# Rounding, remainders, routing steps and the final sums of a mixture-of-experts kernel put in other places

## The reference, cut to what matters

```python
x = x + L0_attn_ref(_layernorm(x), w_qkva, gamma)      # x: 4 x 1024 x 256, float32
#   h = rmsnorm(x, gamma); q, kv, a = split(h @ w_qkva.T, 3); y_t = sigmoid(a_t) * y_{t-1} + kv_t; q * y
x = x + L0_ffn_ref(_layernorm(x), router_w, w_gate, w_up, w_down, sw_gate, sw_up, sw_down)

def _L0_ffn_ref(x, ...):                                # 7 routed experts, top 2; hidden 1024
    logits = x_flat @ router_w.T                        # x_flat: 4096 x 256
    top_vals, top_idx = jax.lax.top_k(logits, 2)
    top_w = jax.nn.softmax(top_vals, axis=-1)
    combine = jnp.sum(jax.nn.one_hot(top_idx, 7) * top_w[..., None], axis=1)
    routed_out = _swiglu(x_flat, w_gate, w_up, w_down)  # down(silu(x @ gate) * (x @ up)), each expert
    mixed = jnp.einsum('end,ne->nd', routed_out, combine)
    return mixed + jnp.mean(_swiglu(x_flat, sw_gate, sw_up, sw_down), axis=0)
```

## Time and profile before

| | |
|---|---|
| device time, median of 3 runs | 1114.69 us (1114.1 to 1115.27) |
| the profiled execution | 1114.16 us, its span 1112.4 us |
| mean granted TensorE clock | 0.965 |
| busy: PE, PEld | 1019.9 us (92%), 882.9 us (79%) |
| busy: DVE, ACT, POOL | 637.9 us (57%), 477.9 us (43%), 407.6 us (37%) |
| DMA over the span | 155.08 MB, mean 139 GB/s |

### The profile page before, as it was taken

One profiled execution on the slowest core, in us unless ns is written; L12 is line 12 of the kernel. 1 busy time (PEld: TensorE's weight loads), 2 busy tenths in 40 slices (PEclk: granted clock), 3 DMA queues, 4 the chain that ended last, 5 costly groups with the idle time before them and its releaser, 6 DMA issues.

```text
span 1112.4 us, 16252 instructions
## 1 busy us (share of the span) xinstructions
PE 1019.9 (92%) x5757; PEld 882.9 (79%) x5757; DVE 637.9 (57%) x1037; ACT 477.9 (43%) x778; POOL 407.6 (37%) x258
## 2 busy tenths in 40 slices
PE   7999999998999999999999999999999688888897
PEld 6788978877989978777877887787779677777776
DVE  7997677876333353464346444644553655656566
ACT  4554342231233244354435443543454444455474
POOL 3234000002101443554455345634653666445300
PEclk9999999999999999999999999999999988888899
DMA  8324110002865744424443444344434555343544
GB/s 293 95 77 113 41 28 10 20 1 82 255 246 179 269 158 166 152 85 160 165 142 94 165 160 141 95 165 165 133 96 168 175 214 198 132 155 118 180 143 142
DMA packets 145907, 155.08 MB, mean 139 GB/s; under 512 B 75321, under 2 KB 134210, under 8 KB 138690
## 3 DMA queue, kind: packets, MB, share of 16 engines
q1 hardware_dynamic: 139120, 136.08, 37.5%
q0 software_dynamic: 6720, 18.36, 5.1%
q10 hardware_dynamic: 18, 0.01, 0.0%
HBM read 127.67 MB, written 26.74 MB: 139 GB/s over the span
## 4 chain that ended last, share of the span: by engine, by line
PE 49%; DVE 23%; ACT 15%; issue 10%; DVEq 0%; DMA 0%; POOL 0%; SPq 0%; ACTq 0%
PE ps L1127 16%; PE ps L1146 9%; DVE ps L1700 7%; DVE w_both L1661 6%; PE ps L1105 5%; PE ps L1083 5%; PE ps L1166 4%; ACT w_both L788 4%; ACT h_hi L849 3%; PE ps L990 3%; ACT silu L844 3%; PE ps L1108 3%; PE ps L1174 2%; ACT silu L816 2%; DVE y_sb L1312 2%
## 5 line engine op out<-in xcount | busy, mean ns | idle before, releaser
L1127 PE MATMUL ps<-xs_hi,w_both 128*128 128x512 f32 x1216 | 402.8, 405 | 41.4 <-DVE ps L1700 33.5
L1127 PEld LDWEIGHTS ps<-xs_hi,w_both 128*128 128x128 f32 x1216 | 236.2, 194 | 108.1 <-DVE ps L1700 49.6
L618 POOL TENSOR_TENSOR w_both<-w_raw,w_both 128x2048 fp32r<-128x2048 f32 x45 | 227.3, 5058 | 95.0 <-ACT w_both L788 86.3
L1127 PE MATMUL ps<-xs_lo,w_both 128*128 128x512 f32 x608 | 243.4, 400 | 0.0
L1700 DVE TENSOR_TENSOR ps<-ps,silu 128x512 f32<-128x512 f32 x160 | 111.3, 696 | 191.8 <-ACT silu L844 135.4
L642 POOL DMA_INDIRECT x_stage<-z_rows,idx_x x70 | 82.1, 1173 | 296.4 <-DVE idx_x L1625 143.8
L1706 DVE TENSOR_TENSOR h_lo<-ps,h_hi 128x512 fp32r<-128x512 f32 x160 | 110.7, 692 | 106.9 <-ACT h_hi L849 85.5
L1105 PE MATMUL ps<-w_both,h_hi 128*128 128x512 f32 x464 | 165.5, 399 | 1.8 <-DVE h_lo L1706 1.8
L1083 PE MATMUL ps<-xs_hi,w_both 128*128 128x256 f32 x640 | 130.1, 303 | 32.8 <-DVE w_both L1661 32.0
L849 ACT ACTIVATE h_hi<-ps 128x512 fp32r<-128x512 f32 x128 | 76.6, 598 | 146.4 <-DVE ps L1700 146.4
L1083 PEld LDWEIGHTS ps<-xs_hi,w_both 128*128 128x128 f32 x640 | 110.6, 210 | 35.5 <-issue 35.4
(11 more groups left out here) (222 smaller groups left out, 1166.2 us busy)
## 6 DMA issues: line engine op xcount, KB each, us to landing
w_raw<-in_L_ffn_w_up_dram SPq DMA_DIRECT2D x20, 1024.0 KB, 4.9
w_raw<-in_L_ffn_w_gate_dram SPq DMA_DIRECT2D x20, 1024.0 KB, 7.1
w_raw<-in_L_ffn_w_down_dram SPq DMA_DIRECT2D x20, 1024.0 KB, 5.5
sorted_rows<-x_stage SPq DMA_DIRECT2D x32, 256.0 KB, 2.2
x_rows<-sorted_rows SPq DMA_DIRECT2D x128, 64.0 KB, 1.9
w_spare<-in_L_ffn_w_up_dram SPq DMA_DIRECT2D x6, 1024.0 KB, 5.2
w_spare<-in_L_ffn_w_gate_dram SPq DMA_DIRECT2D x6, 1024.0 KB, 8.7
w_spare<-in_L_ffn_w_down_dram SPq DMA_DIRECT2D x6, 1024.0 KB, 9.6
```

What stands on the lines that cost most here:

```text
L618: pool.tensor_tensor(w_lo[buf][:, k, :], w_raw[buf][:, k, :], w_hi[buf][:, k, :].bitcast(F32), ALU.subtract).then_inc(wlo_ready[k], 1)
L1127: last = pe.matmul(ps[:, 2 * (j % 2) + part, :], w[:, part, kd * H + j * P:kd * H + (j + 1) * P], xx[:, h // 2, kd, :], start=i == 0, stop ...
```

## The change

It has four parts.

1. **Weights.** ScalarE rounds between silu and the wait for the cast, gate first, then up; in a quad at j = 0, 1, 3 and 4, in a slot at each p. Down is rounded behind the last step. SP loads gate before up. VectorE's two halves of the up remainder stand behind the last step (j = 7) instead of behind j = 3 and 4. GpSimd's first remainder stands before the gathers instead of behind the first.
2. **Routing steps.** They are placed anew between the steps of quads 2 to 8, and `take_lists` and `take_targets` go to quad 8, which keeps its gated product in SBUF (`early=True`) as the others do. SP loads x for LATE between the first two lones' weights.
3. **Lists.** One number, `p + 128 * (tile mod 16) + 1` in float16, takes the place of two bfloat16 values. A list product has 70 columns instead of 140, in one of four column groups by 16 tiles; `take_lists` adds 2048 for each group and sums them.
4. **Mixing.** VectorE mixes the own tiles of each lot, and the others of lot 0, with one multiply-add for each row and choice. ScalarE weighs only the others of lots 1 and 2, and GpSimd adds these. Stores and loads of SP are ordered to match.

```diff
@@ sync @@
-                for k in (1, 0):
+                for k in (0, 1):
                     sp.dma_start(parts_of(w_raw[b])[k], sources[k]).then_inc(raw_in[b][k], 16)
...
             sp.wait_ge(routed, 1)
-            for i in range(2):
-                load_lone(i)
+            load_lone(0)
             for u in range(2):
                 load_x(LATE + u, SA - 2 + u, z_dram, u)
+            load_lone(1)
...
-            for j in range(SBN):
-                if j + 2 < SBN:
-                    sp.wait_ge(mixed, MIX_FROM[j + 1])
-                    load_got(j + 2)
-                store(j)
+            sp.wait_ge(mixed, TOP * (ST + OTHERS[0]))
+            store_others(0)
+            load_got(2)
+            store_own(0)
+            sp.wait_ge(mixed, TOP * (ST + OTHERS[0] + ST))
+            load_got(3)
+            store_own(1)
+            for j in (1, 2):
+                sp.wait_ge(others_mixed, FROM[j + 1] - FROM[1])
+                store_others(j)
+            for j in (2, 3):
+                store_own(j)
@@ gpsimd @@
             for r in range(QUADS):
                 i = NS + 2 * r
+                split_lo(0, r + 2, 1 - r % 2)
                 gather_ahead(i + 4)
-                split_lo(0, r + 2, 1 - r % 2)
                 gather_ahead(i + 5)
                 split_lo(2, r + 2, 1 - r % 2)
...
             for r in range(QUADS, TURNS):
                 i = NS + QUADS + r
+                split_lo(0, r + 2, 1 - r % 2)
                 if i + 4 < NS + ROUTED:
                     gather_ahead(i + 4)
-                split_lo(0, r + 2, 1 - r % 2)
                 split_lo(2, r + 2, 1 - r % 2)
                 scatter_y(i)
+            for j in (1, 2):
+                for b in range(2):
+                    many = OTHERS[j] // 2
...
+                    pool.wait_ge(weighed, TOP * done)
+                    pool.tensor_tensor(sums, sums, got[:, j % 2, ps_, 1, :], ALU.add).then_inc(others_summed, many)
+                    pool.wait_ge(others_summed, done)
+                    pool.tensor_tensor(rows, rows, sums, ALU.add).then_inc(others_mixed, many)
@@ scalar, slot @@
+                    if nxt is not None:
+                        round_w((0, 0, 1, 1)[p], nxt[0], nxt[1], p % 2)
                     act.wait_ge(gated, q + 3)
...
-                    if nxt is not None:
-                        round_w((1, 1, 0, 0)[p], nxt[0], nxt[1], p % 2)
@@ scalar, quad @@
+                    if nxt is not None and j in (0, 1, 3, 4):
+                        round_w(j // 3, nxt[0], nxt[1], j % 3)
                     act.wait_ge(gated, q + 3)
...
-                    if nxt is not None and j < 6:
-                        round_w((1, 1, 0, 0, 2, 2)[j], nxt[0], nxt[1], j % 2)
...
+                if nxt is not None:
+                    for half in range(2):
+                        round_w(2, nxt[0], nxt[1], half)
...
-            quad(NB0, NB0 % 4, between={4: lambda: weigh(0, range(0, 2)), 5: lambda: weigh(0, range(2, 4)),
-                                        6: lambda: weigh(0, range(4, 6))})
-            for p in range(0, 12, 4):
-                weigh(1, range(p, p + 4))
+            quad(NB0, NB0 % 4, between={6: lambda: weigh(1, (ST,)), 7: lambda: weigh(1, (ST + 1,))})
+            weigh(1, range(ST + 2, ST + OTHERS[1]))
             quad(NB0 + 2, (NB0 + 2) % 4, turns=(), between={
-                j: lambda j=j: weigh(2, range(2 * j - 2, 2 * j)) for j in range(1, 7)})
-            weigh(3, range(2))
+                j: lambda j=j: weigh(2, (ST + j,)) for j in range(JH)})
+            weigh(2, range(ST + JH, ST + OTHERS[2]))
@@ tensor @@
-                    last = pe.matmul(ps[:, 7, 0:2 * COLS], hot_lo[:, c % 2, i, :],
...
+                    g = c * GT // 16
+                    last = pe.matmul(ps[:, 7, g * COLS:(g + 1) * COLS], hot_lo[:, c % 2, i, :],
+                                     hot_val[:, c % 2, i, :], start=c * GT % 16 == 0 and i == 0,
...
-                at = {2: {}, 4: {1: [0], 6: [1], JH: [2]}, 6: {1: [3], 2: [4], 6: [5], JH: [6, 7]}, 8: {}}[n]
+                at = {2: {}, 4: {1: [0], JH: [1]}, 6: {0: [2], 1: [3], 6: [4], JH: [5]}, 8: {0: [6], 2: [7]}}[n]
@@ vector @@
-                step(dve.tensor_scalar(hot_val[:, c % 2, :, 0, :], hot_hi[:, :, :], lane[:, 0:1], None,
-                                       ALU.mult))
...
+                listed_ps = ps[:, 7, 0:GROUPS * COLS].rearrange("p (g c) -> p g c", c=COLS)
+                step(dve.scalar_tensor_tensor(out=in_groups[:, :, :], in0=listed_ps, scalar=0.0,
+                                              in1=GROUP_AT.unsqueeze(2).broadcast_to([P, GROUPS, COLS]),
+                                              op0=ALU.is_gt, op1=ALU.mult))
+                step(dve.tensor_tensor(in_groups[:, :, :], listed_ps, in_groups[:, :, :], ALU.add))
+                step(dve.tensor_reduce(rows_f[:, 0, :], in_groups[:, :, :].rearrange("p g c -> p c g"), AX_X, ALU.add))
...
             def mix(j, ps_):
...
+                for k in range(TOP):
+                    for i, p in enumerate(ps_):
+                        if k:
+                            dve.wait_ge(mixed, first_of + i + 1)
...
+                        dve.scalar_tensor_tensor(out=row, in0=got[:, u, p, k:k + 1, :],
+                                                 scalar=mix_w[:, k, t:t + 1], in1=row,
+                                                 op0=ALU.mult, op1=ALU.add).then_inc(mixed, 1)
...
-                    if nxt is not None and j in (3, 4):
-                        split_half(*nxt, j - 3)
+                    if nxt is not None and j == JH - 1:
+                        split_up(*nxt)
...
             betweens = {
+                2: {0: pair_targets, 3: lone_places, 6: lone_targets, 7: find_pairs, "down": move_all,
+                    "half": first_lists},
+                4: {0: lambda: hot_rows(1), 3: lambda: hot_cols(1), 7: lambda: pick(1),
+                    "down": lambda: (halves_of(1), lists(2)), "half": lambda: lists(3)},
+                6: {0: lambda: hot_rows(4), 3: lambda: hot_cols(4), 6: lambda: hot_rows(5), 7: lambda: hot_cols(5),
+                    "down": lambda: (lists(6), owners()), "half": lambda: lists(7)}}
...
-            quad(n, n % 4, turns=ahead_of(n), kind="lone", shared=n, skip=0)
+            quad(n, n % 4, shared=n, early=True, skip=0, between={
+                3: take_lists, 6: take_targets, "down": lambda: turn(n, n % 4, 2, loads(n + 2), 0, "lone"),
+                "half": lambda: turn(n, n % 4, 3, loads(n + 3), 0, "lone")})
...
             quad(NB0, NB0 % 4, turns=ahead_of(NB0), shared=SA, between={
+                6: lambda: mix(0, (0,)), 7: lambda: mix(0, (1,)), "down": lambda: mix(0, range(2, 6)),
+                "half": lambda: mix(1, (0, 1))})
             quad(NB0 + 2, (NB0 + 2) % 4, shared=SA + 2, between={
+                4: lambda: mix(2, (0,)), 5: lambda: mix(2, (1,)), 6: lambda: mix(3, (0,)), 7: lambda: mix(3, (1,))})
```

More of the change, by code:

```diff
@@ L62, in preln_scan_moe_kernel @@
     assert FROM[SBN] == T0
-    MIX_FROM = [j * ST + FROM[j] for j in range(SBN + 1)]
+    assert OTHERS[0] <= 4 and OTHERS[3] == 0
     CHUNKS = TOP * TILES // GT
@@ L207, in preln_scan_moe_kernel @@
         DESC, NUMBERS = iota_f[:, 0:EP], iota_f[0:1, EP:EP + TURNS]
-        assert EP + TURNS <= 48
+        GROUP_AT, VALUES = iota_f[:, 40:40 + GROUPS], iota_f[:, 48:64]
+        assert EP + TURNS <= 40 and GROUPS <= 8
         logits = sb("logits", [P, TILES, EP])
@@ L875, in _ @@
                 quad(n, n % 4, early=True)
-            quad(FIRST_LONE - 2, (FIRST_LONE - 2) % 4, turns=())
+            quad(FIRST_LONE - 2, (FIRST_LONE - 2) % 4, turns=(), early=True)
             for i in range(2):
@@ L879, in _ @@
             quad(LATE, LATE % 4, turns=())
-            lone(2, between={p: lambda p=p: round_w((1, 1, 0, 0)[p], 0, loads_of(0, 0), p % 2) for p in range(4)})
+            lone(2, between={p: lambda p=p: round_w((0, 0, 1, 1)[p], 0, loads_of(0, 0), p % 2) for p in range(4)})
             lone(3, between={p: lambda p=p: round_w(2, 0, loads_of(0, 0), p) for p in range(2)})
@@ L1057, in list_part @@
                 for i in range(GT):
-                    last = pe.matmul(ps[:, 7, 0:2 * COLS], hot_lo[:, c % 2, i, :],
-                                     hot_val[:, c % 2, i, :, :].rearrange("p v c -> p (v c)"),
-                                     start=c == 0 and i == 0, stop=c == CHUNKS - 1 and i == GT - 1)
+                    g = c * GT // 16
+                    last = pe.matmul(ps[:, 7, g * COLS:(g + 1) * COLS], hot_lo[:, c % 2, i, :],
+                                     hot_val[:, c % 2, i, :], start=c * GT % 16 == 0 and i == 0,
+                                     stop=(c + 1) * GT % 16 == 0 and i == GT - 1)
                 last.then_inc(hot_used, 1)
@@ L1608, in hot_cols @@
                                        ALU.is_equal))
[L1609 to L1612 removed]
+                at = c * GT % 16
```

(28 more changed lines are left out.)

78 lines of the change are left out of this document (35 added, 43 removed).

## The result

The changed kernel takes 1053.31 us (median of 4 runs, 1052.41 to 1054.59), against 1114.39 for the kernel before (4 runs, 1112.65 to 1115.27): the ratio is 0.9455, with a 95% interval of 0.9438 to 0.9471, so 61 us or 5.5% faster. The profiled execution has a span of 1051.6 us, 60.8 less than the 1112.4 before. The forecast was 1038, in a range of 1012 to 1066: the direction came out, and of the four terms the quads came out within 0.2 us, the front within 1 and the slots within 5; the tail did not.

The account below looks back on a forecast made before the run. TensorE was taken as the bound, stopped by other engines in quads and slots. Against 1114.16 us the terms -53.4 (quads), -31 (slots), +3 (front) and +5 (tail) summed to -76.4, so 1038, range 1012 to 1066.

Parts of the forecast that it names:

- Routed quads: -53.4: Twelve routed quads: each loses 4.45 us to the up remainder held by GpSimd's; all of it goes, 53.4 us off.
- rival (e): Routed quads: the load loop rules them too; slower, with gate landing at 45 by 24 us, 1138; chance 0.03.
- (d): Routed quads: they keep 1 to 4 us each by a stop not seen; 1050 to 1086; chance 0.13.
- Paired slots: -31: Eight paired slots: stops vanish, but a load loop of about 22 us holds some; 156.7 against 187.66, 31 us off.
- Rival (b): Paired slots: the load loop does not hold them, since something lands earlier; 19 us less, 1019; chance 0.1.
- Rival (c): Slots no load holds: GpSimd wins the 0.2 us race, TensorE stops 4.3 and runs slow 1.5; 1061; chance 0.15.
- Routing and lists: +3: Front to first lone slot: time freed is given back by late lists and weights; 299 against 296.33, 3 us later.
- Tail: +5: Last two quads: 14 us lost to GpSimd's adds where 9 was to be won, so 5 us longer.
- exclusion by turns: Tail: VectorE's multiply-adds and GpSimd's adds exclude each other, the waiting one going next; each turn holds VectorE 2.84 us.
- free path: Last two quads without crowding by ScalarE's weighing and VectorE's pairs: 33.2 and 33.2 + 4.3, 9 us off.
- the stop for the late load: Tail: late load_got(2) holds ScalarE in weigh and TensorE 2.6 us more.
- Rival (a): Tail: its VectorE and GpSimd instructions do not exclude each other; 14 us less, 1024; chance 0.2.

Follow-up runs that it names:

- up_late: Kernel before with one edit: in routed quads VectorE's two up remainders stand behind the last rest instead of behind j = 3 and 4; 1067.39 us, ratio 0.9583.
- round_inside: Kernel before with weights rounded between silu and cast in quads and slots, old order of weights, remainders where they were; 1142.67 us, ratio 1.0245.
- load_first: Changed kernel with SP issuing the next gate and up ahead of the put and x loads in the paired slots; 1027.88 us, ratio 0.9226.
- slots_gather: Changed kernel with the gather put back ahead of GpSimd's first remainder in the paired slots alone; 1064.34 us, ratio 0.9548.
- tail_old: Changed kernel with the mixing part (weighing, multiply-adds, GpSimd's adds, stores) put back as before; 1034.79 us, ratio 0.9282.
- tail_noadds: Changed kernel without GpSimd's eight adds, 20 of 32 tiles of mixed rows left as they were; 1035.81 us, ratio 0.9296.
- lone_first: Changed kernel with the first lone slot's weights loaded ahead of puts and sorted-row loads, the second's behind the four puts; 1054.88 us, ratio 0.9478.

## Why the prediction was right, and where it was not

**Routed quads: -53.4, measured -53.6.** The loss per quad was read rightly and goes whole. Of the two causes given, the place of the up remainder is worth 47.7 (up_late), and the remaining 5.9 come with the rounding between silu and cast and the new order of weights, which were not run apart on top of it; alone, the rounding gives the quads nothing (round_inside). The gate load is issued 27.6 us into the quad (424.79; 27 was worked out), no load holds them, and rival (e) is out, as is (d).

**Paired slots: -31, measured -26.** The mechanism was right: load_first, which moves the weights' issue alone, takes all of the loss. The loop's size was a little off: 22 us a turn were forecast; the first silus of slots 1 to 5 lie 25.2, 23.6, 22.0 and 22.2 us apart, 23.2 in the mean. The first turn begins later than worked out (gate issued 22.6 us into slot 0, not 21.1), since GpSimd has to wait 4.68 us for a scatter of the last quad before slot 0's remainder. Rival (b) is out. Rival (c) is out for the changed kernel: VectorE's halves take 2.35 together in all nine places. In the one that starts at 880.45 the second half starts at 881.58 and GpSimd's down remainder at 881.78:

```profile
881.58 1.22 DVE L1693 TENSOR_TENSOR w_both<-w_raw,w_both 128x1024 fp32r<-128x1024 f32 x1
...
881.78 5.48 POOL L627 TENSOR_TENSOR w_both<-w_raw,w_both 128x2048 fp32r<-128x2048 f32 x1 [1.26 <-ACT w_both L809]
```

VectorE is 0.2 us ahead, as was worked out, and this margin matters: where GpSimd came first, TensorE waited up to 6.9 us (slots_gather) and 7.4 us (round_inside) before the next slot, and these slots took 9 to 10 us more than 17.2, not the 5.8 of (c).

**Routing and lists: +3, measured +4.** idx_x was ready at 270.9 (274 forecast) and the weights were issued at 287.11, where 16.2 behind idx_x was taken. TensorE waited 9.1 for them (7 forecast) and ran slow behind it (9.76 us for 64 matmuls that take 7.1 at full clock; 1.5 forecast, 2.6 measured); the routing steps and list parts before it gave back some 2 us more than was counted.

**Tail: +5, measured +14.8.** This is the step that failed. The mechanism, exclusion by turns, was right; the terms were not. "With a free path they are 33.2 and 33.2 + 4.3 for add and store: 9 us off": the path is not free with either mixing. With the old one the two quads take 77.46 us, without GpSimd's adds 78.48, so no more than 1 to 2 of the 9 were to be won. What tail_old wins is 2.2 us of TensorE's busy time: before the change NB0 ran at clock 0.94, behind the last slot's stop. A load of gathered rows that ScalarE must weigh before its next silu stops TensorE 5.18 us even with no adds.

From that free path, 70.7 us, 14 were to be lost; 23.9 were (94.57 in all). The first stop was 5.77, where 5 was worked out, and the further turn 1.42 instead of 3. Too small were the stop for the late load (2.6 against 4.63) and the slow clock (3 against 6.6: TensorE is busy 73.0 us with matmuls taken at 66.4, at a clock of 0.85 in the last quad). Two terms stood at nothing: a wait of 1.5 us for `h_lo`, which is there before the change too, and 3.9 at the end. "The stores now stand behind load_got in SP's queue, which the last matmuls cover" holds for the first stores alone; the last three wait for GpSimd's last add. Against tail_noadds the adds cost 16.1 us: 6.6 in stops, 4.6 in slow clock and 4.9 at the end. Rival (a) is out by tail_noadds.

The misses of slots and tail, 5 and 10 us, had the same sign, and with 1 of the front the time came out 15 above the forecast.

## What to carry to other kernels

An in-order queue of transfers puts its own order into every loop that passes through it: a weight load that waits for a gather that waits for the last weight load is a ring, and the place to cut it is the queue, where the two have nothing to do with each other; cutting it at the busy engine cost 11 us here and cutting it at the queue won 25. When two engines exclude each other, moving work to the second helps only where the first has nothing of that kind to do; note for each such pair which one comes first, as 1.5 us of order was worth 3.4 us a slot. A stretch that is taken to be free once the known stop is gone should be checked for the next wait before it is booked as a gain. And work that is handed to a less busy engine should be followed to the last store: here it ended behind the last matmul and cost 4 us there.

## What the runs showed that was not expected

Which of the two goes next isn't always by turns, as the prediction had read it. In the earlier trace rows GpSimd went between VectorE's two halves, and in round_inside a waiting half went between GpSimd's two remainders (its first half took 4.6 us). In slots_gather, four times out of four, a half that had waited since 809.72 was passed by GpSimd's second remainder, which started right behind its first at 812.52, and took 8.4 us. What decides between the two I did not find.

With a load of 3 MB issued beside the indirect gathers, these took longer in the one trace that has it (lone_first): the first put behind a gather came at 279.10 instead of 275.19, so that bringing a late load forward by 15 us gained nothing.
